# A bias row as a product with ones, a second bank for the second sum, and attention's fill products in two halves

## What is computed

```python
def _L1_ffn_ref(x, U1, V1, U2, V2, b1, b2):          # rank 128, inner width 1376
    P = jnp.einsum('bsh,hr->bsr', x, U1)
    H = jnp.einsum('bsr,rf->bsf', P, V1) + b1
    gate, up = (H[..., :INTER], H[..., INTER:])
    act = jax.nn.silu(gate) * up
    Z = jnp.einsum('bsi,ir->bsr', act, U2)
    return jnp.einsum('bsr,rh->bsh', Z, V2) + b2
...
x = x + 0.5 * _L0_ffn_ref(_layernorm(x), ...)
x = x + _L0_attn_ref(_layernorm(x), ...)
x = x + 0.5 * _L0_ffn_ref(_layernorm(x), ...)
x = x + 0.5 * _L1_ffn_ref(_layernorm(x), ...)
x = x + _L1_attn_ref(_layernorm(x), ...)             # 32 heads of 16, causal, 4 batches of 256
x = x + 0.5 * _L1_ffn_ref(_layernorm(x), ...)
```

## Time and profile before

| | us |
|---|---|
| Median of 3 runs | 1828.55 (1826.43 to 1830.91) |
| The profiled execution | 1826.44 |
| Its span in the trace | 1824.70 |
| PE busy | 1745.2 (96%) |
| DVE / ACT / POOL busy | 1110.3 / 1084.2 / 929.4 |
| Mean granted clock of PE | 0.994 |

### The profile page before, as it was taken

How to read it: one execution, slowest core, us unless ns; L and a number is a source line. 1 busy time by engine, 2 the same in 40 slices (tenths; PEclk the granted TensorE clock), 3 DMA queues, 4 the chain that set the end, 5 groups by cost and what they waited for, 6 DMA issues and landing times.

```text
span 1824.7 us, 32143 instructions
## 1 busy us (share of the span) xinstructions
PE 1745.2 (96%) x11088; PEld 1517.0 (83%) x11088; DVE 1110.3 (61%) x3318; ACT 1084.2 (59%) x3075; POOL 929.4 (51%) x1170
## 2 busy tenths in 40 slices
PE   7989999999999999999999999999999988899788
PEld 6779999999998998999899999899887766666566
DVE  6665465456456546545654654564656777777657
ACT  3355566566557656656755655665553454777954
POOL 5555445555445555545555445555523355678740
PEclk9999999999999999999999999999999999999999
DMA  4300011012002001101200210120011121000001
GB/s 150 109 20 7 19 59 36 1 47 64 1 18 70 25 1 59 53 1 30 64 18 7 70 35 1 35 70 7 18 58 41 41 69 36 2 2 19 25 7 47
DMA packets 35424, 65.78 MB, mean 36 GB/s; under 512 B 4032, under 2 KB 4672, under 8 KB 35264
## 3 DMA queue, kind: packets, MB, share of 16 engines
q1 hardware_dynamic: 35264, 63.73, 11.2%
HBM read 61.62 MB, written 2.10 MB: 35 GB/s over the span
## 4 chain that ended last, share of the span: by engine, by line
PE 74%; ACT 7%; DVE 7%; issue 6%; POOL 5%; DMA 0%; POOLq 0%; SPq 0%; DVEq 0%; ACTq 0%
PE bank L362 58%; PE bank L1037 6%; PE bank L1024 4%; PE bank L1039 3%; ACT s L1151 2%; POOL s L1900 2%; ACT s L1655 1%; PE bank L1598 1%; PE bank L1569 1%; POOL h L774 1%; DVE h L709 1%; PE bank L1585 1%; DVE work L1256 1%; POOL rstd L327 1%; ACT pt L1648 1%
## 5 line engine op out<-in xcount | busy, mean ns | idle before, releaser
L362 PE MATMUL bank<-W,oT 128*128 128x512 f32 x1632 | 430.5, 400 | 0.0
L1362 POOL TENSOR_TENSOR qk<-work,qk 128x512 fp32r<-128x512 f32 (+1 forms) x160 | 192.9, 1205 | 429.8 <-ACT qk L1142 429.8
L362 PEld LDWEIGHTS bank<-W,oT 128*128 128x128 f32 x1632 | 288.7, 189 | 47.7
L1158 ACT COPY pt<-bank 128x384 f32<-128x384 f32 x256 | 122.0, 477 | 323.9 <-PE bank L1024 323.3
L1354 POOL TENSOR_TENSOR work<-work,table 128x512 f32<-128x512 f32 (+1 forms) x160 | 191.3, 1196 | 134.2 <-ACT work L1137 134.2
L1151 ACT ACTIVATE s<-s,neg_max 128x128 f32<-128x128 f32 (+1 forms) x512 | 227.6, 445 | 50.2 <-DVE neg_max L1270 49.0
L362 PE MATMUL bank<-W,xnA 128*128 128x320 f32 (+1 forms) x1056 | 187.3, 334 | 4.0 <-DVE xnA L347 3.4
L362 PEld LDWEIGHTS bank<-W,xnA 128*128 128x128 f32 x1056 | 167.2, 188 | 18.0 <-DVE xnA L347 4.6
L1247 DVE TENSOR_TENSOR work<-bank,table 128x512 f32<-128x512 f32 (+1 forms) x160 | 101.9, 637 | 129.1 <-ACT work L1137 129.1
L362 PE MATMUL bank<-qk 128*128 128x256 f32 (+1 forms) x768 | 166.0, 351 | 0.9 <-POOL qk L1362 0.9
L1290 DVE COPY lvv<-bank 128x320 f32<-128x320 f32 x128 | 62.8, 491 | 169.9 <-PE bank L362 169.5
(11 more groups left out here) (106 smaller groups left out, 3502.6 us busy)
## 6 DMA issues: line engine op xcount, KB each, us to landing
raw<-in_weights SPq DMA_DIRECT2D x215, 256.0 KB, 2.7
x<-in_x SPq DMA_DIRECT2D x8, 256.0 KB, 4.9
out<-x SPq DMA_DIRECT2D x8, 256.0 KB, 2.3
row<-in_bias_rows SPq DMA_DIRECT2D x5, 256.0 KB, 2.7
table<-in_constants SPq DMA_DIRECT2D x4, 240.0 KB, 3.2
b_qk<-in_bias_rows SPq DMA_DIRECT2D x1, 512.0 KB, 4.5
b_val<-in_bias_rows SPq DMA_DIRECT2D x1, 256.0 KB, 3.0
table<-in_constants SPq DMA_DIRECT2D x1, 66.0 KB, 2.3
```

Of the source, the lines that this page charges most:

```text
L362: last = nc.tensor.matmul(out_ap, lhs(i), rhs(j), start=start and k == 0, stop=stop and k == 2)
L1158: nc.scalar.copy(pt0[:, k, :], bank[PT][:, 0:3 * P]).then_inc(a_pt, 1)
L1362: nc.gpsimd.tensor_tensor(lo, work[:, 2 + s, st.columns(what)], hi.bitcast(F32), ALU.subtract).then_inc(a_rope_lo, 1)
```

## The change

In layer 1's feed-forward the bias row is split once for each pass into a tile `row_parts`, high part in partitions 0 to 63 and low part in partitions 64 to 127, and each output tile gets it by a fourth matmul with `row_ones`, which is 1 in two partitions and 0 elsewhere. The 8 additions on DVE go. The second half's sum Z is made in bank 7, the output tiles take other banks, and DVE makes the low part of the norm ahead of tiles out, statistics and scaling. In attention, the fill product of a step is cut into two halves of 6 matmuls, the first before turns 2 and 3, the second after them, unless the step before has transposed a tile of the norm; in these steps DVE copies head 3 after the first reciprocal and not before it. There are 19 such steps (n = 2, 3, 4, 7, 10 to 15, 18 to 24, 29, 30).

```diff
-        RING, LNB, ZB, FIRST_Z = (0, 1, 2), 3, 4, 2
+        RING, LNB, ZB, FIRST_Z = (0, 1, 2), 3, (4, 7), 2
+        ROW_AT = 5
+        row_parts = chunk(W, G_CHUNKS - 1)[HI]
+        row_ones = chunk(W, G_CHUNKS - 1)[LO][:, 0:P]
+        REST = slice(P // 2, P)
...
-                self.out_banks = (4, 5, 6, 7) if layer == 0 else (5, 6, 7)
+                self.out_banks = (4, 5, 6, 7) if layer == 0 else (5, 6, 5, 6, 4, 5, 6, 4)
...  # added(t)
+                if self.layer:
+                    return self.x_before + 1 + t
...  # tensor_out
+                b = self.bank_of(self.o0 + o)
                 if t == 0:
                     pe.wait_ge(pz_lo, self.z0 + 2 + k + 1)
-                if o >= 3:
-                    pe.wait_ge(x_written, self.added(o - 3))
+                    pe.wait_ge(f_row_lo, self.rows_made)
+                if b in self.out_banks[:o]:
+                    pe.wait_ge(x_written, self.added(max(p for p in range(o) if self.out_banks[p] == b)))
                 at = F1_COLS - DIM
-                product(bank[self.bank_of(self.o0 + o)][:, :],
-                        lambda i: pz[i][:, k, t * P:(t + 1) * P],
-                        lambda i: self.w[i][:, at:at + DIM]).then_inc(f_out, 1)
+                product(bank[b][:, :], lambda i: pz[i][:, k, t * P:(t + 1) * P],
+                        lambda i: self.w[i][:, at:at + DIM], True, False)
+                nc.tensor.matmul(bank[b][:, :], row_ones, row_parts,
+                                 start=False, stop=True).then_inc(f_out, 1)
...  # tensor_down
-                    if first and k == 1:
-                        pe.wait_ge(pz_lo, self.z0 + 3)
-                    last = product(bank[ZB][:, :], self.down(m), lambda i: self.h[i][:, q % 2, :],
+                    last = product(bank[ZB[k]][:, :], self.down(m), lambda i: self.h[i][:, q % 2, :],
                                    first, end)
...  # FFN.scalar, after the high parts of the norm
+                    if self.layer and i == ROW_AT:
+                        act.wait_ge(row_loaded, 16 * (self.row_n + 1))
+                        nc.scalar.copy(row_parts, row[:, :]).then_inc(f_row_hi, 1)
...  # FFN.vector, after L720
+                    for n, t in self.ln_tiles(k, m - 3) if self.layer else []:
+                        ln_lo_part(dve, n, LNB, xn_tile(t))
                     for t in self.tiles_out(i):
                         add(t)
...
+                    if self.layer and i == ROW_AT + 1:
+                        if self.rows_made == 1:
+                            nc.vector.tensor_tensor(row_ones, ident[:, 0:1].to_broadcast([P, P]),
+                                                    ident[:, P // 2:P // 2 + 1].to_broadcast([P, P]), ALU.add)
+                        dve.wait_ge(f_row_hi, self.rows_made)
+                        nc.vector.tensor_tensor(row_parts[REST, :], row[REST, :],
+                                                row_parts[REST, :].bitcast(F32),
+                                                ALU.subtract).then_inc(f_row_lo, 1)
-                    if M - 4 <= m < M:
+                    if not self.layer and M - 4 <= m < M:
                         t = 4 * k + m - (M - 4)
...
-                    for n, t in self.ln_tiles(k, m - 3) if self.layer else self.turns(i):
+                    for n, t in [] if self.layer else self.turns(i):
                         ln_lo_part(dve, n, LNB, xn_tile(t))
...
-        X3, X4 = X2 + 2 * TILES, X2 + 4 * TILES
+        X3, X4 = X2 + 2 * TILES, X2 + 3 * TILES
...  # b_tensor_project and b_tensor_out take the part of their four chunks
+        WHOLE, FRONT, REAR = range(KC), range(KC // 2), range(KC // 2, KC)
...  # b_tensor_step
+            halves = fill_of(n) and n >= 1 and not norm_of(n - 1)
+            if halves:
+                fill(FRONT)
             if n >= 1:
                 turn(n - 1, 2)
                 turn(n - 1, 3)
             if fill_of(n):
-                kind, b, i = fill_of(n)
-                fill_released(pe, (kind, b, i))
-                if kind == "proj":
-                    b_tensor_project(pe, b, i)
-                else:
-                    b_tensor_out(pe, b, i, bank[FILL])
+                fill(REAR if halves else WHOLE)
...  # b_vector_step
-            if before:
+            halves = fill and before and not norm_of(n - 1)
+            if before and not halves:
                 b_pt_copy(dve, n - 1, 3)
             if here:
                 inverses(0)
+            if halves:
+                b_pt_copy(dve, n - 1, 3)
```

## The result

| | before | after |
|---|---|---|
| Median (least to greatest), us | 1829.73 (1826.43 to 1831.44), 4 runs | 1816.41 (1814.86 to 1938.90), 4 runs |
| Ratio, 95% interval | 1 | 0.9926 [0.9912, 0.9940] |
| Profiled execution / its span | 1826.44 / 1824.7 | 1814.88 / 1812.9 |
| PE busy | 1745.2 | 1745.1 |

A forecast was written before the change was run, and what follows sets the result against it. PE, busy 96% of the span, was taken to bound the kernel, with waits mostly for DVE. Passes 7.0 + 1.25, together 8.3, plus attention 4.2 make 12.5 us: 1828.55 - 12.5 = 1816.0 us, range 1810 to 1823.

The forecast's parts named there:

- first wait: PE's 1.71 us wait for a normed tile's low part, first pass: 0.5 left, gain 1.2; second pass's 1.57 gains 1.35.
- second: PE's 1.47 us wait in the first pass: low part no longer behind a row addition of 0.68, gain 0.6.
- third, and its clock: First pass, 3.00 us wait for the split of Z: gain 1.7, 1.3 remaining; half the clock's loss regained, 0.8.
- fourth, and its clock: First pass, 3.13 us wait: PE waits for the scaled tile, 1.4 left, gain 1.7; clock stays up, gain 1.5.
- fifth and last: First pass: 1.06 us wait for h's low part falls to about 0.2, gain 0.86; the last, 0.71, stays.
- products with ones: Eight more matmuls a pass on PE at 0.227 us each: cost 1.36 in the first pass, 1.81 in the second.
- Attention: First halves cover 6.5 us of waits ahead of turns 2 and 3; 19 extra entries cost 2.2; gain 4.2.
- Margin of the second half: Attention's halved steps: the moved copy ends 0.4 us before PE reaches the product with the values.
- Waits handed on: Rival: feed-forward DVE waits only change place and the clock still falls; passes give 3.4 us, total 1821; chance 0.18.
- Halves for nothing: Rival: extra entries or POOL's scaling take back the halves' gain in attention; 8.3 us in all, 1820; chance 0.16.
- More than forecast: Rival: both clocks stay high, first wait goes, shorter steps free DVE; gain 17 us, 1811; chance 0.10.
- The other side: Rival: second half too short, so 19 attention steps wait ahead of the product with the values; 1835 at 1.0 us; chance 0.05.

The follow-up runs named there:

- Kernel 7: The change with POOL's and ACT's splits of attention's weights begun at i = 13 in place of 9; 1815.2 us, ratio to before 0.9925.
- kernel 9: The change with DVE splitting Z ahead of h at i = 13 and PE making output tiles ahead of down products; 1816.3 us, ratio to before 0.9942.
- kernel 4: The change with DVE's low part of the norm again behind tiles out, statistics and scaling; 1815.4 us, ratio to before 0.9934.
- kernel 3: The change with the bias row added by DVE again and no product with ones; 1818.3 us, ratio to before 0.9946.
- kernel 6: The change without the 16 matmuls with ones, so the bias row is left out of the result; 1812.6 us, ratio to before 0.9916.
- kernel 1: The kernel before with attention's halved fill products alone; 1823.1 us, ratio to before 0.9975 [0.9965, 0.9985].
- kernel 11: The change with the last pass's weight splits in attention at steps 21 to 30 in place of 20 to 29; 1812.2 us, ratio to before 0.9915.
- kernel 8: The change with the fill product cut into 9 and 3 matmuls in place of 6 and 6; 1819.4 us, ratio to before 0.9954.
- kernel 12: The change with later weight splits in attention, Z split ahead of h, and outputs first at i = 22 only; 1812.0 us, ratio to before 0.9891.
- kernel 2: The kernel before with the feed-forward part of the change alone; 1820.4 us, ratio to before 0.9958 [0.9943, 0.9972].

## Why the prediction was right

The total came out as forecast, with the second pass, but luck has a part in it: the first pass gave 1.7 us less than its 7.0 and attention 1.6 more than its 4.2, for reasons that have nothing to do with each other.

**First pass: 7.0 forecast, 5.3 measured.** The measured column is by how far PE is ahead at the same piece of work, counted from the start of the stage, so it holds the small waits too:

| term | forecast | measured |
|---|---|---|
| first wait | 1.2 | 2.0 |
| second | 0.6 | 0.5 |
| third, and its clock | 1.7 + 0.8 | 1.7 together |
| fourth, and its clock | 1.7 + 1.5 | 2.3 + 1.1 |
| fifth and last | 0.9 + 0 | -0.8 |
| products with ones | -1.36 | -1.5 |

The step that failed is what is left of the waits for DVE's low parts, in two places. The third wait was to be 1.3 us and is 2.60. The gain of 1.7 came all the same: 0.68 by the down product that now stands ahead of the wait, some 0.6 by a split that comes sooner, and the rest by small waits (0.17 and 0.22 before it) that went, so that PE came sooner too and waits the longer. But the clock fell as before, and its 0.8 did not come. I had the split come 0.9 us earlier, as DVE is without a row addition. It came 0.6 earlier (13.05 us behind the end of the second wait, where it was 13.64): the addition's 1.66 us were in part filled by a new wait of 0.73 for ACT ahead of the low part of h, and the two low parts behind it take 1.80 and 1.76 beside POOL's splits. Kernel 7, with short low parts, shows that these make the wait; kernel 9 shows that the order alone takes it to 1.40.

At the fifth, what was forecast came ("about 0.2 is left": 0.16 ahead of the last down product). What the sum did not have is the wait of 1.25 one down product earlier, where the kernel before had none: counted from the start of the stage, PE came there 7.0 us sooner, but the low part of h that it needs began only 5.6 sooner (1494.21 for 1499.19) and took 1.35 beside POOL. In the sum I had given the row's additions the price beside POOL and the low parts the price without it, though the trace shows that either pays it. The prediction's own sign of being wrong, low parts that end waits of over 2 us, is there: L786, which ends the 2.60, is the low part of Z.

The first wait was better than forecast. VectorE's timeline of the changed kernel there:

```profile
1451.39 0.69 DVE L756 TENSOR_TENSOR W<-row,W 64x512 fp32r<-64x512 f32 x1
...
1452.78 0.68 DVE L347 TENSOR_TENSOR xnB<-bank,xnB 128x512 fp32r<-128x512 f32 x1
1453.38 0.54 DVE L322 TENSOR_SCALAR work<-x,mean_var,rstd 128x512 f32<-128x512 f32 x1
```

The split of the row (L756), the one feared new instruction, cost 0.69. POOL's split of h came second, from 1451.77, and took 1.47 where 1.29 is its usual length. Then DVE's instructions that read PSUM run while POOL works, and the scaling comes after it and takes 0.54, not 1.28. The low part in the earlier trace rows, which the prediction took as near POOL's work, began only after it (1454.62; POOL had ended at 1454.14); this one, at 1452.78 and still 0.68, shows that such a low part is not held. The order is not the sole cause at this place: the first wait is gone in kernel 4, with the old order, and in kernel 3, with the additions. Where the order shows its use is the fourth wait (0.77 for 1.46 in kernel 4). The rule of the Trainium skill (SBUF — State Buffer, Who interferes with whom), that of two such instructions the later one waits for the other, agrees with 1.47 for 1.29 here and with the low part of h, 1.80 us in the change and 0.69 in kernel 7.

**Fourth wait: right**, in mechanism and place. PE waits for the scaled tile, 0.77 us where 1.4 was forecast, since the scaling takes 0.78 and not 1.28, and the granted clock is 1.00 behind it. The reason given for the clock, that a wait of 1.4 us is below one of 1.57 that let it stay, does not hold: in kernel 9 it fell behind a wait of 1.40, and in attention of the kernel before behind one of 1.48 (at 1526.16).

**Second pass: 1.25 forecast, 1.3 measured.** 1.57 became 0.32, 1.46 became 0.86, and 1.09 went, as forecast. A wait of 0.58 for a low part of h is new; the products cost 1.3 net and not 1.81 (kernel 6). The two misses cancel.

**Attention: 4.2 forecast, 5.8 measured** by the starts of PE's first products, and 5.9 by the steps at a full clock; kernel 1's ratio gives 4.6, and its interval, 1.8 us to either side, allows the forecast as well as these. The mechanism is right and the size of a wait was wrong. An ordinary step went from 6.43 to 5.89, 0.54 less, where the sum had 0.33 less 0.12. In the kernel before, turns 0 and 1 begin at 1595.22 and turns 2 and 3 at 1596.42, 1.20 us later; without a wait the same transposes take 0.63 (1587.96 to 1588.59 above). So the listed wait of 0.33 cost 0.57. Turns 2 and 3 then took 0.66 and take 0.57 behind matmuls. Against these 0.66 us stands the cut: twelve matmuls took 2.91 (1597.08 to 1599.99) and the two sixes take 1.47 and 1.57, 0.13 more, as the sum had it (0.12). That leaves 0.53. Left out altogether was step 22 (0.9 us, kernel 11), where the first half stands before a bank that is not yet free. In steps 13 and 21 a wait of 0.24 is left ahead of turn 3.

**Margin of the second half: right in an ordinary step.** 0.4 us by the sum, 0.5 to 0.6 by kernel 8. But in steps 3, 11 and 19 PE waits 0.30 us ahead of the product with the values, which the prediction named as a sign of being wrong; it cost little, as these steps still gained 0.37.

**The rivals.** *Waits handed on* holds in part: the third wait kept most of its length and its fall of the clock, and a new one came ahead of the fifth. *Halves for nothing* fell by kernel 1. *More than forecast* fell in the change; kernel 12, with three more edits, comes to 20 us by its ratio (1830.76 x 0.0109). *The other side* needs 9 and 3 to show.

**What stays open.** Where the clock falls, and why in attention by the estimate more often in the kernels with halves (4.7 to 11.8 us) than in the two without (6.1 and 3.2). The lengths themselves come out. Before and kernel 2 have the same attention, and the steps in which only the one or only the other lost its clock account for the 2.7 us between them: 0.8 ahead of the first product with the values, 0.9 in step 7, 1.1 in step 26 and 1.5 at the end, less 1.2 in step 6 and 0.3 in step 29. In the same way falls of the clock are some 1.8 of the 2.3 us between kernels 11 and 12, which have the same attention.

## What to carry to other kernels

An elementwise instruction next to a busy GpSimd has two prices, and all of its neighbours pay them as well: when a sum takes the high price for what goes, it must take it for what stays. Cut work that covers a wait so that each piece is longer than the wait behind it, but look at what the front piece itself needs (a bank, a tile) and at who frees it. The instructions of other work in an engine's order (here POOL's splits of weights for later use) decide how long a split or a sine is waited for: moving them by one step took 2.7 us from step 22, more than the halves had taken from any other.

## What the runs showed of the hardware that was not expected

The clock is not set by the code alone. The profiled executions of the change and of kernel 11 have the same code and the same third wait in the first pass. PE's timeline and the window behind it, in kernel 11:

```profile
1472.16 0.98 PE L362 MATMUL bank<-WF,W 128*128 128x512 f32 x3 [2.60 <-DVE W L786]
```

```profile
1472.10:1476.20 4.10, 4.04 (x18) 3.31 (x19) 2.70 (x5) 2.34 (x4) 1.36 (x2) 1.00 0.40 123
```

Here the clock stayed at 1.00 behind 2.60 us of waiting, and it fell to 0.59 in the change behind the same 2.60. Kernel 6 kept it at 1.00 too, while kernel 7 lost it behind a wait of 2.05 us and kernel 9 behind one of 1.40. In the first pass of the code before it took 3.4 us in one execution and 7.7 in another, by the estimate. A stage of one trace can be compared with another only after this is taken out.

The second thing is the listed wait: behind a group of transposes 0.33 us in the list was 0.57 us of time, from start to start.

The third is how little a fall of the clock can cost: 1.1 us in step 26 and 0.3 in step 29 of attention without halves, where busy time times the missing clock gives about 1.6.
